# A two-stage conditioned recurrence on one core: its start-up rearranged, the bias of the rank factors turned on TensorE, the first state taken from the early bank

## What is computed

```python
# layer 0: a base matrix plus a rank-8 matrix made from the condition
ae  = layernorm(cond) * ln_g + ln_b
h   = gelu(ae @ w1 + b1)                # 256
xw  = h @ w2 + b2                       # 4096: x_a and x_b, each (256, 8)
layer = base_layer + einsum('bdr,bkr->bdk', x_a, x_b)
y   = x + (x + x @ layer)               # = 2x + x @ layer
# layer 1: a tanh recurrence over 1024 steps, h0 = cond
h_t = tanh(h_{t-1} @ Wh + (y_t @ Wx + b))
out = y + h
```

## Time and profile before

| | us |
|---|---|
| median of 3 runs | 765.58 |
| lowest, highest | 765.46, 765.87 |
| the profiled execution, its own time | 765.27 |
| its span, first to last instruction | 762.8 |
| TensorE products, busy | 689.1 (90%) |
| ScalarE, busy | 498.6 (65%) |
| VectorE, busy | 282.3 (37%) |

### The profile page before, as it was taken

The page is one execution under the profiler, slowest core; times in us unless marked ns, Lnnn a source line. Parts: engine busy times, 40 slices in busy tenths (PEclk is TensorE's granted clock), DMA queues, the critical chain, the costliest instruction groups (busy, mean ns, idle before and its releaser), DMA issues.

```text
span 762.8 us, 45964 instructions
## 1 busy us (share of the span) xinstructions
PE 689.1 (90%) x18799; PEld 622.8 (82%) x18799; DVE 282.3 (37%) x1543; ACT 498.6 (65%) x5143; POOL 7.5 (1%) x19
## 2 busy tenths in 40 slices
PE   4899999999999999999999999999999999999997
PEld 4688888888888888888888888888888888888886
DVE  6533333333333333333333333333333333333332
ACT  6566666666666666666666666666666666666665
POOL 3000000000000000000000000000000000000000
PEclk9755555555555555555555555555555555555555
DMA  8000000000000000000000000000000000000000
GB/s 284 6 7 9 11 11 9 12 6 9 11 12 9 11 7 9 11 11 9 11 7 9 11 11 9 11 9 7 11 11 9 11 11 5 11 11 9 7 7 6
DMA packets 12285, 12.36 MB, mean 16 GB/s; under 512 B 1813, under 2 KB 11056, under 8 KB 12080
## 3 DMA queue, kind: packets, MB, share of 16 engines
q1 hardware_dynamic: 11984, 9.45, 4.3%
q0 software_dynamic: 96, 0.02, 0.0%
HBM read 7.36 MB, written 2.10 MB: 12 GB/s over the span
## 4 chain that ended last, share of the span: by engine, by line
PE 77%; ACT 19%; issue 2%; DMA 1%; DVE 0%; SPq 0%; DVEq 0%; another core or an unknown queue 0%
PE acc L330 49%; ACT h_pre L498 19%; PE pre L330 14%; PE pre L310 4%; PE p_w L294 4%; PE p_w L289 2%; PE p_w L284 1%; PE acc L414 1%; DMA w_f<-w_dram 1%; PE pre L307 1%; PE pre L440 0%; PE p_w L435 0%; SPq L220 0%; SPq L225 0%; SPq L228 0%
## 5 line engine op out<-in xcount | busy, mean ns | idle before, releaser
L330 PE MATMUL acc<-h_pre,wh_s 128*128 128x2 f16 x8192 | 384.7, 168 | 58.6 <-DVE acc L626 0.7
L498 ACT ACTIVATE h_pre<-pre 128x2 f16<-128x2 f32 x2046 | 240.8, 170 | 249.2 <-PE pre L330 249.2
L330 PEld LDWEIGHTS acc<-h_pre,wh_s 128*128 128x128 f16 x8192 | 301.5, 106 | 122.2 <-ACT h_pre L498 105.8
L631 DVE TENSOR_TENSOR h_lo<-p_f,h_pre 128x4 f16<-128x4 f32 x1024 | 165.3, 161 | 460.6 <-ACT p_f L504 456.0
L330 PE MATMUL pre<-h_rnd,wh_s 128*128 128x2 f16 x4092 | 270.2, 170 | 0.0
L330 PE MATMUL acc<-h_lo,wh_s 128*128 128x2 f16 x4096 | 257.5, 167 | 0.0
L330 PEld LDWEIGHTS pre<-h_rnd,wh_s 128*128 128x128 f16 x4092 | 190.7, 108 | 0.0
L330 PEld LDWEIGHTS acc<-h_lo,wh_s 128*128 128x128 f16 x4096 | 189.2, 106 | 0.1
L508 ACT ACTIVATE h_f<-acc 128x4 f32<-128x4 f32 x1024 | 186.4, 182 | 0.5 <-PE acc L330 0.5
L506 ACT ACTIVATE h_rnd<-acc 128x4 f16<-128x4 f32 x1022 | 172.8, 169 | 0.0
L504 ACT ACTIVATE p_f<-acc 128x4 f32<-128x4 f32 x1023 | 161.6, 158 | 0.0
(11 more groups left out here) (90 smaller groups left out, 145.0 us busy)
## 6 DMA issues: line engine op xcount, KB each, us to landing
w_f<-w_dram SPq DMA_DIRECT2D x8, 512.0 KB, 7.2
x_in<-x_dram SPq DMA_DIRECT2D x32, 64.0 KB, 2.4
out_dram<-o_row SPq DMA_DIRECT2D x64, 32.0 KB, 2.0
w_f<-w_dram SPq DMA_DIRECT2D x1, 256.0 KB, 5.0
base_f<-base_dram SPq DMA_DIRECT2D x1, 256.0 KB, 9.4
wh_f<-wh_dram SPq DMA_DIRECT2D x1, 256.0 KB, 9.6
wx_f<-wx_dram SPq DMA_DIRECT2D x1, 256.0 KB, 9.9
cond_r<-cond_dram SPq DMA_DIRECT2D x1, 2.0 KB
```

Of the source, the lines that this page charges most:

```text
L330: return nc.tensor.matmul(dst, wh_s[:, pw, ki, mo * P:(mo + 1) * P], h[:, par, ki, :], start=False, stop=True, skip_group_check=True)
L498: nc.scalar.activation(h_pre[:, n % 2, m, :], src, func, scale=scale).then_inc(s_hpre[(n // HALF) % 2], 1)
L631: nc.vector.tensor_sub(h_lo[:, par].rearrange("p m b -> p (m b)"), p_f[:, 0:COLS], h_pre[:, par].rearrange("p m b -> p (m b)")).then_inc(s ...
```

## The change

All of it lies in the start-up, the first half-block and the last output row, but for some semaphore clears.

- **b2** is loaded as four rows of 1024 (`b2_q`), turned on TensorE by eight small float32 transposes, and copied by VectorE into the accumulator of the L414 products, which are then added onto it. The sum `ab_sum` goes; one `tensor_reduce` for each batch adds the two parts of the accumulator.
- **Loads**: b1 is issued second by SyncE, ln_g and ln_b by ScalarE, w1 after the first piece of w2, x after the fourth piece.
- **x**: ScalarE makes `x_f` and the high part of x (after its cast of piece 5), VectorE only the low part.
- **Order of the casts**: ScalarE makes the initial state before it casts wx and wh; VectorE makes the low parts of wx and wh in halves (`low(dst, src, k, n)`), at other places of its queue.
- **Identity products**: 16 of 128 columns (`BASE`) instead of 4 of 512, in groups: 4 after the turn of the factors, 6 just ahead of the first half-block, 3 after each of the steps u = 1 and u = 2.
- **x times factor a** in blocks for one batch each; its split is one cast and one subtraction.
- **First half of y on its own**: `y_new0`, `y_high0`, `y_low0` do 16 steps at a time, the second half's split comes at u = 1 of the first half-block; `y_cur` is copied by ScalarE at u = 6.
- **The initial state's products** (the whole of step u = 0) go onto the early bank `pre[A]` (`state_products`), ten of them ahead of the products with y. `first_step` of ScalarE then takes the first state, `h_pre`, `p_f`, `h_f` and `h_rnd`, from `pre[A]`; the step loops of the first half-block begin at u = 1.
- **The layer** (`layer_high` of ScalarE) is cast in four 128 x 256 pieces after the steps u = 1 to 4; VectorE's `layer_low` comes at u = 2 to 5 and waits for two such pieces.
- **Clears**: the seeds' semaphores are cleared after the step and not before it; x's are no longer cleared; the last output row clears none.

```diff
@@ loads and x
-            load_w2(0)
-            for n, v in enumerate((ln_g, ln_b, b1)):
-                sync.dma_start(vec_r[n * NM:(n + 1) * NM, :], v.rearrange("(m p) -> m p", p=P)).then_inc(s_vec, 16)
+            sync.dma_start(vec_r[2 * NM:3 * NM, :], b1.rearrange("(m p) -> m p", p=P)).then_inc(s_vec, 16)
+            load_w2(0)
...
@@ PE, half_steps
-                for u in range(HALF):
-                    if u >= SEED and u < SEED + 2 and not (last and half == B):
-                        take(pe, s_seed[u % 2], 1)
+                for u in range(1 if first else 0, HALF):
+                    seeded = (SEED <= u < SEED + 2 and not (last and half == B)) or (first and u < 3)
+                    if seeded:
+                        pe.wait_ge(s_seed[u % 2], 1)
                     chain_step(half, u, last=last and half == B and u == HALF - 1)
+                    if seeded:
+                        pe.sem_clear(s_seed[u % 2])
+                    if first and u < 3:
+                        summed = base_products(BASE[7 + 3 * u:10 + 3 * u])
+                        if u == 2:
+                            summed.then_inc(s_laysum, 1)
@@ PE, start-up
+            pe.wait_ge(s_b2, 16)
+            for r in range(RANK):
+                nc.tensor.transpose(acc[1][:, 64 + 4 * r:64 + 4 * (r + 1)],
+                                    b2_q[:, :].rearrange("q (p r) -> q r p", r=RANK)[:, r, :], ident[0:4, 0:4])
+            nc.tensor.matmul(acc[0][:, 64:64 + P], ident16[:, :], ab_st[:, 0:2].rearrange("p q b s r -> p (q b s r)"),
+                             start=True, stop=True, skip_group_check=True).then_inc(s_b2turn, 1)
             pe.wait_ge(s_hid, 1)
+            pe.wait_ge(s_b2seed, 1)
...
-            for bb in range(NB):
-                for pw in range(2):
-                    nc.tensor.matmul(pre[B][:, bb, :], ident16[:, :], base_s[:, pw].rearrange("p k n -> p (k n)"),
-                                     start=pw == 0, stop=True, skip_group_check=True)
...
+            base_products(BASE[0:4])
...
             pe.wait_ge(s_bw, 16)
-            input_products(A, INPUT).then_inc(s_fill, 1)
-            for par in range(2):
-                take(pe, s_seed[par], 1)
-            pe.wait_ge(s_split, 2)
+            input_products(A, [product for product in INPUT if product[1] is None])
+            pe.wait_ge(s_hi, 2)
+            pe.wait_ge(s_hpre[A], NM)
+            state_products([(0, mo, ki) for mo, ki in TILES], h_pre)
+            pe.wait_ge(s_hlo[A], 1)
+            state_products([(0, mo, ki) for mo, ki in TILES], h_lo)
+            pe.wait_ge(s_split, 3)
+            state_products([(1, mo, 0) for mo in range(NM)], h_pre)
+            pe.wait_ge(s_yhi0, 1)
+            input_products(A, [product for product in INPUT if product[1] is not None and product[3] == 0])
+            pe.wait_ge(s_ylo0, 1)
+            input_products(A, [product for product in INPUT if product[1] is not None and product[3] == 1])
+            pe.wait_ge(s_split, 4)
+            for mo in range(NM):
+                state_products([(1, mo, 1)], h_pre).then_inc(s_presum[A], 1)
+            base_products(BASE[4:8]).then_inc(s_laysum, 1)
+            base_products(BASE[8:10])
             half_steps(A, first=True)
@@ ScalarE
+            def layer_high(bb, k):
+                act.wait_ge(s_laysum, bb + 1)
+                nc.scalar.copy(lay_s[:, 0, bb, k, :], pre[B][:, bb, k * D:(k + 1) * D]).then_inc(s_layhi, 1)
+            def first_step():
+                act.wait_ge(s_seed[0], 1)
+                for m in range(NM):
+                    give_pre(1, m, pre[A][:, m, 0:NB], ACT.Tanh, 1.0 / SCALE)
...
             def half_block(half, first=False, last=False):
-                for u in range(HALF):
+                for u in range(1 if first else 0, HALF):
...
+                    if first and u <= 2 * NB:
+                        layer_high((u - 1) // NM, (u - 1) % NM)
+                    if first and u == 6:
+                        act.wait_ge(s_yrest, 1)
+                        nc.scalar.copy(y_cur[:, :, :, :].rearrange("p t m b -> p (t m b)"),
...
@@ VectorE
             def layer_low(bb, k):
-                dve.wait_ge(s_layhi, bb + 1)
+                dve.wait_ge(s_layhi, NM * (bb + 1))
...
             def half_steps(half, first=False, last=False):
-                for u in range(HALF):
+                for u in range(1 if first else 0, HALF):
                     chain_step(half, u)
-                    if first and u < 2 * NB:
-                        layer_low(u // NM, u % NM)
+                    if first and u == 1:
+                        y_high0(B)
+                        dve.wait_ge(s_yhi0, 2)
+                        y_low0(B, s_yrest)
+                    if first and 2 <= u < 2 + 2 * NB:
+                        layer_low((u - 2) // NM, (u - 2) % NM)
...
+            xa = acc[1][0:NB * 4 * RANK, 0:NB * BLOCK].rearrange("p (b t) -> p b t", b=NB)
+            linked(nc.vector.tensor_copy(xa_s[:, 0], xa))
+            nc.vector.tensor_sub(xa_s[:, 1], xa, xa_s[:, 0]).then_inc(s_xas, 1)
+            low(wh_s, wh_f, 0, 2)
+            dve.wait_ge(s_ymm, 1)
+            linked(y_new0(A))
+            y_high0(A)
+            dve.wait_ge(s_yhi0, 1)
+            y_low0(A, s_ylo0)
+            low(wh_s, wh_f, 1, 2)
+            y_new0(B).then_inc(s_link, 1)
+            dve.sem_clear(s_ymm)
+            dve.wait_ge(s_presum[A], NM)
+            for par in (1, 0):
                 seed(A, par)
-            keep_y()
+            dve.wait_ge(s_link, count[0] + 1)
             half_steps(A, first=True)
```

More of the change, by code:

```diff
@@ L205, in cond_recurrence @@
         TILES = [(mo, ki) for mo in range(NM) for ki in range(NM)]
+        BASE = [(bb, c, pw) for bb in range(NB) for c in range(2 * NM) for pw in range(2)]
         FILL, FIRST_FILL, LAYERS, SEED = 2, 6, 8, 10
@@ L280, in _, with turn_out @@
         def _(pe):
+            turned = [0]
             def turn_x():
-                take(pe, s_xload, 16)
+                turned[0] += 1
+                pe.wait_ge(s_xload, 16 * turned[0])
                 nc.tensor.transpose(p_w[:, 0:P], x_in[:, :], ident[:, :]).then_inc(s_xturn, 1)
-            def turn_out():
-                take(pe, s_osum, 1)
+            def turn_out(last=False):
+                pe.wait_ge(s_osum, 1)
+                if not last:
+                    pe.sem_clear(s_osum)
                 nc.tensor.transpose(p_w[0:HALF * COLS, 0:P], o_sum[:, :], ident[:, :]).then_inc(s_oturn, 1)
@@ L316, in share, with base_products, state_products @@
                 return todo[k * n:(k + 1) * n]
+            def base_products(todo):
+                for bb, c, pw in todo:
+                    cols_c = slice(c * P, (c + 1) * P)
+                    last = nc.tensor.matmul(pre[B][:, bb, cols_c], ident16[:, :],
+                                            base_s[:, pw].rearrange("p k n -> p (k n)")[:, cols_c],
+                                            start=(bb, c, pw) == BASE[0], stop=True, skip_group_check=True)
+                return last
+            def state_products(todo, h):
+                for pw, mo, ki in todo:
+                    last = nc.tensor.matmul(pre[A][:, mo, 0:NB], wh_s[:, pw, ki, mo * P:(mo + 1) * P], h[:, 0, ki, :],
+                                            start=False, stop=True, skip_group_check=True)
+                return last
             def clear_states(half):
@@ L428, in _ @@
             py = p_w[:, P:2 * P].rearrange("p (m c) -> p m c", m=NM)
[L429 to L430 removed]
+            pe.wait_ge(s_xsplit, 1)
             pe.wait_ge(s_baselo, 1)
@@ L491, in _ @@
             half_steps(B, last=True)
-            turn_out()
+            turn_out(last=True)
         @block.scalar
@@ L517, in half_block @@
                             give_pre(n, m, pre[half][:, m, u * NB:(u + 1) * NB], ACT.Tanh, 1.0 / SCALE)
-                    act.wait_ge(s_sum[half], u + 1)
+                    act.wait_ge(s_sum[half], u if first else u + 1)
                     give_h(n, acc[u % 2][:, z_cols(half, u)], ACT.Tanh, 1.0 / SCALE,
@@ L560, in _ @@
             give_h(0, cond_c[:, :], ACT.Copy, 1.0)
+            high(wx_s, wx_f, s_wx)
+            high(wh_s, wh_f, s_wh)
             for n, side in enumerate((1, 0)):
@@ L564, in _ @@
                                pre[A][0:NB * 4 * RANK, n, 0:NM * P]).then_inc(s_abts, 1)
-            for bb in range(NB):
-                act.wait_ge(s_lmm, bb + 1)
-                nc.scalar.copy(lay_s[:, 0, bb].rearrange("p k n -> p (k n)"), pre[B][:, bb, :]).then_inc(s_layhi, 1)
+            first_step()
             half_block(A, first=True)
@@ L578, in _ @@
             px = p_w[:, 0:P].rearrange("p (t m b) -> p m b t", m=NM, b=NB)
+            turned = [1]
             def keep_x():
-                take(dve, s_xturn, 1)
+                turned[0] += 1
+                dve.wait_ge(s_xturn, turned[0])
```

(19 more changed lines are left out.)

118 lines of the change are left out of this document (57 added, 61 removed).

## The result

The changed kernel takes **768.28 us** (median of 7 runs, 767.25 to 768.72) against 765.46 for the kernel before on the same chip (7 runs, 764.81 to 765.91): a ratio of 1.0034, 95% interval 1.0024 to 1.0044. It is slower by 2.8 us; 763.7 was predicted, and even the slow end of the range, 764.8, is 3.5 us too low.

What follows compares the result with a forecast made beforehand. Bound: the serial step chain through TensorE and ScalarE, where a late `h_lo` delays the next step. -3.36 + 0.26 + 1.46 - 0.22 = -1.86 from 765.27 gives 763.41 profiled; median 0.31 above, 763.7 us (762.3 to 764.8).

Steps and rivals of the forecast that it cites:

- The seeds' clears: Seeded steps of all half-blocks: the clears move from before a step to after it, one for one; 0 us.
- if a later half-block's steps change: Sign that the forecast is wrong: after the first half-block, steps were to stay at 0.714 us to the end.
- The start-up: Up to the recurrence's first `h_pre`: it comes at 25.1 instead of 28.46, -3.36 us, loads included.
- The rival of a start-up that gives 1.0 less: Half of y is not really on its own, so the start-up gains 1.0 less: 764.7 us; chance 22%.
- the second side of the factors: Start-up: ready at 21.70 instead of 21.95, 0.26 us off, as one wait and `ab_sum` go.
- The turns of b2: Start-up: eight turns, 1.0 us in all, hidden in the 2.80 that TensorE idles before the w2 products.
- The loads: Start-up: the changed order lands w2's third piece 0.2 us earlier, between 0.5 earlier and 0.3 later.
- The third rival: Loads crowd each other and w2's third piece lands late; from 1.9 us late the change loses; chance 5%.
- The stalls: First half-block, u = 2 and 4: `layer_low` waits for a later piece, delaying `h_lo`; +1.46 us (1.1 to 1.8).
- The identity products in the steps: First half-block, u = 1 and 2: three products and a clear add 0.13 a step, +0.26 us (0.05 to 0.5).
- The trace grants 1.00 in the stretch of L440: Start-up clock: granted 1.00, yet 0.43 us per 512-column product means 1.2 GHz; rank-8 products priced at that level.
- The last row: Last output row: TensorE's clear and VectorE's two leave the chain, -0.22 us (0 to -0.3).

Runs made afterwards that it cites:

- e1: The changed kernel with the seeds' semaphores waited for and cleared ahead of the step again, as before the change; 762.54 us, ratio 0.9962.
- e2: e1 plus a wait on the long-met bias-load semaphore between the seeds' clear and the step; 768.21 us, ratio 1.003.
- e5: The kernel before, with only the seeds' semaphores waited for ahead of the step and cleared behind it; 770.76 us, ratio 1.0074.
- e6: The changed kernel with the two waits ahead of the step swapped, `h_pre`'s written first, then the seeds'; 762.85 us, ratio 0.9968.
- e3: e1 plus a clear of an unused semaphore behind the seeded steps; 762.83 us, ratio 0.9966.
- e4: e1 with each of VectorE's `layer_low` one step later, at u = 3 to 6; 761.36 us, ratio 0.9942.
- e7: e4 with loads in the old order: ln_g, ln_b, b1 behind the first piece of w2, x behind the second; 761.88 us, ratio 0.9955.
- e9: e4 with eight identity products ahead of the steps, two each behind u = 1 and 2, and w2's first piece issued before b1; 761.38 us, ratio 0.9949.
- e4_again: e4 unchanged, run once more beside e9 on the same chip; 761.06 us, ratio 0.9944.
- e8: e4 with the identity products again in one block of four times 512 columns, none in the steps; 762.74 us, ratio 0.997.

## Why the prediction was wrong

**The step that failed: "The seeds' clears move from before a step to after it, one for one, in all half-blocks: 0."** I counted the clears and did not look at what the one ahead of the step carried. Moving it put two waits next to one another, in two steps of every half-block. Each such step is 0.047 longer and each u = 12 behind them 0.007 shorter, which makes 0.174 in 32 steps (23.007 against 22.833 in e1). Over the 990 steps that is 5.28 (711.87 against 706.59 in e1), and 0.18 more in the first 32: 5.5 us where I had 0. Against before it shows as 5.02 (706.85), because the change also gives 0.2 in those steps that I had not counted: the step with the turn of x, which lost its clears, takes 0.727 where it took 0.733. e2, e5 and e6 show the two waits from three sides, and e3 excludes the clear. My text had the test for it, "if a later half-block's steps change", but no rival and no price for these steps. It did have a price two sentences on, where the last row is worked out with "a plain hand-over is 0.05 and two waits 0.1"; with two such steps in each of 63 half-blocks, 0.05 is 6 us. No plain step of before has two neighbouring waits, so its trace gave no warning.

By the medians 4.6 are missing between the 763.7 predicted and the 768.28 measured, less than the 5.5 of this step. The rest of the change came out better than forecast, as e1 shows: 762.54 without the step. Of those 1.2 us 0.65 is time outside the span, for which I had taken over a profiled execution of before with much of it, and 0.31 is what I had added on top of that execution: about 1 us that has nothing to do with the change.

**The start-up.** From the cast of the third piece to the first `h_pre` I had 25.1 - 10.17 = 14.93; it is 14.89 in after, and 14.9 behind the landing in e1, e2, e3, e4, e7, e9 and e4_again. The rival of a start-up that gives 1.0 less is out. In e6 it is 15.36, and its timeline shows why:

```profile
11.30 0.62 DVE L822 TENSOR_TENSOR hid_s<-hid,hid_s 128x4 f16<-128x4 f32 x1 [0.80 <-ACT hid L613]
```

This small operation of VectorE, for which the w2 products wait, takes 0.16 in the other eleven traces. Here it lay beside an operation of GpSimd (L277, 11.24 to 11.90) and ended 0.02 behind it, 0.46 late. That GpSimd's operation is what held it up is my reading; no run was made for it. Inside, the second side of the factors was 11.53 behind the cast by my count, and is 22.49 - 11.20 = 11.29; L497 was 12.63 behind it and is 12.46. The four identity products between the turns and L497 lie in the 0.5 us in which TensorE waits for `ab_t` anyway. The turns of b2 (five of the eight take 0.71, from 9.43) stay under the 2.43 that TensorE idles ahead of the w2 products.

**The loads.** I took 0.2 earlier; the cast came 0.83 later than in the execution of before, beyond the 0.3 of my bound. Against the forecast that is 1.03, and it is all of the 0.99 by which the first `h_pre` is later than predicted. e7 leaves open how much of it is the order. What is shown is a spread of 1.6 us from one execution to another among kernels with the same order but for b1 in e9, and it enters the time one for one (the 14.9 above); a term of 0.2 was finer than this transfer repeats. The third rival (loads against the change, from 1.9 us late) did not happen.

**The first half-block.** The stalls: 1.46 predicted; 1.420 - 0.713 = 0.71 and 1.467 - 0.713 = 0.75, **1.46**, and they come behind the two `layer_low` named, those of u = 2 and u = 4. e4 takes them away and the time with them. The Trainium skill ("TensorE: Matmul & The Clock Gate", Architectural detail) says that VectorE's queue is strict FIFO, and the trace agrees: `h_lo` started 0.74 late, queued behind an operation that it does not need. The identity products in the steps: 0.26 predicted, 0.13 for each of two steps. e1 shows 0.03, 0.06 and 0.03 over the plain step at u = 1 to 3, 0.12 in all, but e8, which has no identity product there, still has 0.739 and 0.732 at u = 1 and 2. The products themselves are the difference of e4 and e8, 0.04 at u = 2 and 0.03 at u = 3: the idle 0.24 takes nearly all three. What else lengthens u = 1 and 2 was not looked into.

**The clock.** The view by stretch shows 1.00 for the 990 steps of after and 0.50 for those of before, yet the plain step is 0.713 in both. Executions of before shown with 0.52 took 765.42 and 765.19 us, others shown with 1.00 took 765.12 and 765.14. The trace of after holds no record of the clock at all, so its 1.00 is a missing record and no measurement. The Trainium skill ("TensorE: Matmul & The Clock Gate", The HAM clock gate) warns that the trace's events of the gate have been seen to be unreliable, and this case agrees. It also undoes a reading in the prediction: "The trace grants 1.00 in the stretch of L440". The first record in the trace of before is at 23.57 us, behind that stretch; it has 1.00 from there to 26.99, then 0.50. The 0.43 for a product of 512 columns came from its durations and stands: that is 1.2 GHz.

Behind the block the clock was at its upper level (2.4 GHz) in before too, and the rank-8 products took 0.39 there, as in e8:

```profile
25.15 0.39 PE L473 MATMUL pre<-ab_t 32*128 32x256 f16 x4
```

In after they take 0.61. The same section's rule, that dense products release the clock, agrees with this, and with the 0.22 that e8 has off them. But the block costs 0.94 in the start-up net of that, so my choice, to price the rank-8 products at the lower level, was the right one for this change.

**The last row.** -0.22 predicted, -0.31 measured. Timeline of after, answering to the earlier trace rows:

```profile
763.63 0.22 DVE L689 TENSOR_TENSOR o_sum<-y_cur,h_f 128x64 f32<-128x64 f32 x1 [0.57 <-ACT h_f L555]
...
763.92 0.42 PE L296 MATMUL p_w<-ident,o_sum 128*64 128x128 f32 x1 [0.52 <-DVE o_sum L689]
764.37 0.28 DVE L698 COPY o_row<-p_w 64x128 f32<-64x128 f32 x1 [0.51 <-PE p_w L296]
```

From the end of `o_sum` to the turn it is 0.07 (0.15 before), from its end to the copy 0.03 (0.24 before).

**The account.** 763.41, the predicted profiled execution, plus 0.99 (first `h_pre`), 0.03 (first 32 steps: 0.18 for the waits, 0.15 less for the rest of them), 5.02 (the other steps), less 0.09 (last row) and 0.65 (outside the span) is 768.71, what it took.

## What to carry to other kernels

In a serial chain look at every instruction between a wait and the first instruction behind it: removing or moving one can leave two waits side by side, and then the one that is met last must be the one that the consumer itself carries (here the one written first), or the hand-over gets 0.05 us longer in every step that has it. Whether a moved clear or wait is free is read from what is left in its old place, not from what is counted in the new one. And an operation on an in-order engine that waits for two things belongs behind the place where the second one is made; here one step later was worth 1.2 to 1.3 us.

## What the runs showed of the hardware that was not expected

Of two waits written one behind the other ahead of one weight load, the last written became an instruction of its own, 51 ns long, on TensorE (after, e2, e6). With `h_pre`'s wait in it the load starts 0.114 us behind the end of `h_pre`, without it 0.051. A clear takes 56 ns on TensorE, with a wait in it (before) or without (e3), and two steps of each half-block with a clear behind their products are no longer for it (e3, 22.833 in 32 steps).

The third load of 512 KB landed between 9.58 and 11.30 us in twelve profiled executions, three with the old order of loads and nine with the new one. Within one execution the 16 DMA engines were done with it between 8.68 and 11.18 in after and between 9.84 and 10.34 in before. This spread of more than 1 us is larger than most terms of the start-up.

A VectorE operation of 128 x 4 elements that takes 0.16 us in eleven traces took 0.62 in e6, beside an operation of GpSimd that ended 0.02 earlier.
